# Probabilities of an attention stage: turned over DRAM and on VectorE instead of TensorE, and a new order of each engine's round

## The reference, cut to what matters

```python
kv_c, q_c = kv @ W_kvc, q @ W_dq
k_rope, q_rope = _rope(kv_c @ W_kr, lk), _rope(q_rope, lq)
scores = (einsum('bhqd,bkhd->bhqk', q_nope, k_nope) + einsum('bhqr,bkr->bhqk', q_rope, k_rope)) * scale
good = (k_ids <= qs) & (k_ids >= qs - LOOKBACK)
attn = softmax(where(good[:, None, :, :], scores, NEG), axis=-1)
out = einsum('bhqk,bkhd->bqhd', attn, v).reshape(b, lq, H * HD)
return out @ W_o
```

## Time and profile before

| | us |
|---|---|
| median of 3 runs | 3070.87 |
| lowest, highest | 3063.78, 3072.26 |
| the profiled execution, its own time | 3065.81 |
| its span in the profile | 3064.0 |
| PE, DVE, ACT, POOL busy in it | 3032.5, 2248.4, 1379.9, 1224.1 |

### The profile page before, as it was taken

One profiled execution on the slowest core, in us unless ns is written; L12 is line 12 of the kernel. 1 busy time (PEld: TensorE's weight loads), 2 busy tenths in 40 slices (PEclk: granted clock), 3 DMA queues, 4 the chain that ended last, 5 costly groups with the idle time before them and its releaser, 6 DMA issues.

```text
span 3064.0 us, 50062 instructions
## 1 busy us (share of the span) xinstructions
PE 3032.5 (99%) x18181; PEld 2636.4 (86%) x18181; DVE 2248.4 (73%) x5504; ACT 1379.9 (45%) x3399; POOL 1224.1 (40%) x1190
## 2 busy tenths in 40 slices
PE   9999999999999999999999999999999999999999
PEld 6777777899899799999999999999998788888887
DVE  7989999755677788888888888888887533333342
ACT  4655555433566455555555555555555211111111
POOL 9999999454333433333222333333311111111120
PEclk9999999999999999999999999999999999999999
DMA  4444442298899511111111111111102211111110
GB/s 153 131 144 138 129 130 86 86 307 299 220 265 284 189 49 49 49 49 43 49 42 49 49 49 36 49 38 47 49 29 81 88 56 55 55 49 43 46 42 14
DMA packets 179011, 292.41 MB, mean 95 GB/s; under 512 B 22616, under 2 KB 73952, under 8 KB 178768
## 3 DMA queue, kind: packets, MB, share of 16 engines
q1 hardware_dynamic: 145200, 193.24, 20.4%
q0 software_dynamic: 23344, 77.35, 7.9%
q10 hardware_dynamic: 10224, 18.62, 1.6%
HBM read 177.38 MB, written 111.76 MB: 94 GB/s over the span
## 4 chain that ended last, share of the span: by engine, by line
PE 92%; DVE 3%; DMA 2%; POOL 1%; ACT 1%; issue 1%; SPq 0%; POOLq 0%; DVEq 0%
PE f_Y L559 4%; PE t_U L1818 4%; PE f_Y L560 4%; PE f_Y L562 4%; PE t_U L1819 4%; PE t_U L1820 4%; PE g_O L2640 4%; PE g_PH L2628 4%; PE g_PH L2627 4%; PE g_PH L2626 4%; PE g_O L2642 4%; PE g_O L2641 4%; PE t_T L1794 3%; PE f_Y L554 2%; PE t_PO L1804 2%; PE t_PO L1805 2%
## 5 line engine op out<-in xcount | busy, mean ns | idle before, releaser
L1954 ACT ACTIVATE t_pr<-t_sm,t_nb 128x256 f32<-128x256 f32 x512 | 256.7, 502 | 418.5 <-DVE t_nb L2176 418.5
L2372 POOL TENSOR_TENSOR t_r<-t_r 128x256 f32<-128x256 f32 x128 | 95.8, 749 | 696.7 <-DVE t_r L2155 387.5
L2696 DVE CAST g_hh<-g_hf 128x512 fp32r<-128x512 f32 x128 | 67.8, 530 | 382.0 <-PE g_O L2642 380.2
L2667 ACT ACTIVATE g_hf<-g_PH,b1g 128x512 f32<-128x512 f32 x128 | 88.1, 688 | 528.3 <-PE g_PH L2628 457.0
L1360 POOL TENSOR_TENSOR c_kf<-c_vt,c_ct 128x512 f32<-128x512 f32 x256 | 284.5, 1129 | 5.9 <-ACT c_vt L775 3.2
L2186 DVE TENSOR_SCALAR t_pr<-t_pr,t_rw 128x256 f32<-128x256 f32 x512 | 256.7, 501 | 18.1
L559 PE MATMUL f_Y<-c_kh,c_th 128*128 128x512 f32 x540 | 250.8, 465 | 0.0
L562 PE MATMUL f_Y<-c_kl,c_th 128*128 128x512 f32 x540 | 213.7, 396 | 0.7 <-DVE c_kl L1072 0.7
L560 PE MATMUL f_Y<-c_kh,c_tl 128*128 128x512 f32 x540 | 213.4, 395 | 0.0
L2640 PE MATMUL g_O<-g_w,g_hh 128*128 128x512 f32 x512 | 200.1, 391 | 5.0 <-DVE g_hl L2698 5.0
L1818 PE MATMUL t_U<-t_voh,t_oth 128*128 128x512 f32 x512 | 202.0, 394 | 0.0
(11 more groups left out here) (375 smaller groups left out, 9974.9 us busy)
## 6 DMA issues: line engine op xcount, KB each, us to landing
xs<-c_zero SPq DMA_DIRECT2D x71, 256.0 KB, 4.6
f_xg<-xs SPq DMA_DIRECT2D x284, 64.0 KB
ys<-f_yt ACTq DMA_DIRECT2D x71, 256.0 KB, 5.1
f_xg<-xn SPq DMA_DIRECT2D x40, 256.0 KB, 4.9
c_xt<-x SPq DMA_DIRECT2D x32, 256.0 KB, 3.5
c_cr<-ctx SPq DMA_DIRECT2D x32, 256.0 KB, 4.0
...
```

## The change

It has these parts.

- PE's `pturn` is gone, with its bank T, which becomes the second bank of PO. The probabilities of head N are normalised by ACT (`normalise(N)`, in ACT's round N+1, a copy scaled by the reciprocal) into `pr` in another order of columns. SP writes them to DRAM (`fp`), waits for that, and reads them back as `pq`. DVE turns them in blocks of 32x32 into `ptq` (`pturn(N)`, in DVE's round N+2). ACT makes `pth` from it. The low part is made by GpSimd for even heads, in its round N+2, and by DVE for odd heads, at the start of its round N+3 (`plow`).
- `av` moves from round N+2 to N+3 on PE, `vo` from N+4 to N+5; `oth` and `otl` have two buffers instead of three, and their ACT and DVE steps move to round N+4.
- In each engine's round the chain of the probabilities comes first. `qabs` of DVE moves from the end of the even round to the odd round behind it.
- The result is stored by SP in four pieces, two rounds later than GpSimd did it, and the residual is loaded in four pieces a round later. The rows come in the order of the turned blocks. x2 of batches 2 and up is kept by GpSimd's queue. GpSimd's mix is spread over rounds 11 to 14.
- `krf` shares memory with `kc`, so DVE's `krope` waits for `kvp`.
- At the seam, the first block of the dense stage (`dense_first(0, 0)`) is put on PE ahead of the last `vo`, the rows of group 1 move two steps earlier on SP, and the first dense weights are split a round later.

The diff, cut to its core:

```diff
 def sync_attention:
+    def store(b):
+        w.wait_ge(*V["add", 2 * b + 1])
+        for c in range(4):
+            sp.dma_start(turned_rows_of(d["x3"][b], c), m.xo[32 * c:32 * c + 32, :, :]).then_inc(*Q["to"]("out", b, c))
+    def probabilities(N):
+        w.wait_ge(*A["nm", 2 * N + 1])
+        w.wait_ge(*V["pt", N - 4])
+        sp.dma_start(d["fp"][N % 4].rearrange("(i p f) -> p i f", i=4, f=128),
+                     m.pr[:, N % 2, :, :, :, :].rearrange("p i k t f -> p i (k t f)")).then_inc(*Q[f"ps{N % 2}"]("ps", N))
+        w.wait_ge(*Q[f"ps{N % 2}"]["ps", N])
+        w.wait_ge(*V["pt", N - 2])
+        sp.dma_start(m.pq[:, N % 2, :], d["fp"][N % 4].rearrange("(p l) -> p l", p=128)).then_inc(*Q[f"pl{N % 2}"]("pl", N))
...
+        if N >= 6 and (N - 6) % NH == NH - 1:
+            store((N - 6) // NH)
+        if 5 <= N < TOTAL and (N - 5) % NH == (12 if N - 5 < NH else 8):
+            residual((N - 5) // NH)
...
+        if N < TOTAL:
+            probabilities(N)
 def tensor_attention:
-    def pturn(N):
-        w.wait_ge(*V["nm", 2 * N + 1])
-        w.wait_ge(*V["ptl", N - 1])
-        for kb in range(2):
-            for t in range(2):
-                i = pe.transpose(m.T[...], m.pr[:, N % 2, t, 128 * kb:128 * kb + 128], ident)
     def av(N):
-        w.wait_ge(*V["ptl", N])
-        w.wait_ge(*V["otl", N - 1])
+        o = m.PO[N % 2][:, 0:256]
+        w.wait_ge(*(V if N % 2 else G)["ptl", N])
+        w.wait_ge(*V["otl", N - 2])
...
+        if N >= 5:
+            vo(N - 5)
...
+        if 3 <= N <= TOTAL + 2:
+            av(N - 3)
+        if N == TOTAL + 2:
+            dense_first(pe, w, K, 0, 0)
 def scalar_attention:
+    def normalise(N):
+        w.wait_ge(*Q[f"ps{N % 2}"]["ps", N - 2])
+        for t in range(2):
+            x, k4 = 2 * N + t, (2 * N + t) % 4
+            w.wait_ge(*V["rc", x])
+            ac.activation(m.pr[:, N % 2, :, :, t, :], m.sm[:, k4, :].rearrange("p (i k f) -> p i k f", i=4, k=2), ACT.Copy,
+                          scale=m.rw[:, k4, 1:2]).then_inc(*A("nm", x))
     def pturn(N):
-        w.wait_ge(*P["pt", N])
+        w.wait_ge(*V["pt", N])
...
+        if 4 <= N <= TOTAL + 3:
+            av(N - 4)
+        if 1 <= N <= TOTAL:
+            normalise(N - 1)
         if N < TOTAL:
             exps(N)
+        if 2 <= N <= TOTAL + 1:
+            pturn(N - 2)
 def vector_attention:
     def pturn(N):
+        w.wait_ge(*Q[f"pl{N % 2}"]["pl", N])
+        w.wait_ge(*P["av", N - 2])
+        ve.transpose(m.ptq[:, N % 2, :, :].rearrange("p k q -> p (k q)").rearrange("p (k c t) -> p c k t", k=4, c=4),
+                     m.pq[:, N % 2, :].rearrange("p (c k f) -> p c k f", c=4, k=4)).then_inc(*V("pt", N))
+    def plow(N):
         w.wait_ge(*A["pth", N])
...
+        if 3 <= N <= TOTAL + 2 and N % 2 == 0:
+            plow(N - 3)
         if N < TOTAL:
             maxima(N)
+        if 2 <= N <= TOTAL + 1:
+            pturn(N - 2)
+        if N < TOTAL and N % 2 and (N + 1) // 2 < TOTAL // 2:
+            qabs((N + 1) // 2)
+        if 4 <= N <= TOTAL + 3:
+            av(N - 4)
...
+            inverses(N)
+        if N >= 5 and (N - 5) % NH == NH - 1:
+            add_rows((N - 5) // NH)
 def gpsimd_attention:
+    def pturn(N):
+        w.wait_ge(*A["pth", N])
+        gp.tensor_tensor(m.ptl[:, N % 2, :, :], m.ptq[:, N % 2, :, :], f32(m.pth[:, N % 2, :, :]), ALU.subtract).then_inc(*G("ptl", N))
...
+        if 2 <= N <= TOTAL + 1 and N % 2 == 0:
+            pturn(N - 2)
```

More of the change, by code:

```diff
@@ L277, in attention_memory @@
     m.pth = t("pth", [128, 2, 2, 256], F32R)
+    with ExitStack() as low:
+        m.ptq = sb(nc, low, "t_ptq", [128, 2, 2, 256])
     m.ptl = t("ptl", [128, 2, 2, 256], F32R)
-    m.oth = t("oth", [128, 3, 256], F32R)
-    m.otl = t("otl", [128, 3, 256], F32R)
+    m.oth = t("oth", [128, 2, 256], F32R)
+    m.otl = t("otl", [128, 2, 256], F32R)
     m.sm = t("sm", [128, 4, 256])
-    m.pr = t("pr", [128, 2, 2, 256])
+    m.pr = t("pr", [128, 2, 4, 2, 2, 32])
+    m.pq = t("pq", [128, 2, 512])
     m.wkh = t("wkh", [128, 2, 128], F32R)
@@ L1553, in every_other_head, with turned_rows_of, kept @@
     return qr[half, q4 % 2, :, :].rearrange("p (i z) c -> p z i c", z=2)[:, z, :, :]
+def turned_rows_of(ap, c):
+    return ap.rearrange("(t u c) l -> u c t l", t=2, c=4)[:, c, :, :]
+def kept(b):
+    return "tx2" if b < 2 else "tx3"
 def halves_of(ap):
@@ L1593, in residual @@
         if b:
-            w.wait_ge(*Q["to"]["out", b - 1])
+            w.wait_ge(*Q["to"]["out", b - 1, 3])
         else:
@@ L1633, in sync_attention @@
     segment(1)
-    for N in range(TOTAL + 4):
+    for N in range(TOTAL + 7):
         b, h = divmod(N, NH)
-        if N >= 4 and (N - 4) % NH == (12 if N - 4 < NH else 8):
-            residual((N - 4) // NH)
+        if N >= 6 and (N - 6) % NH == NH - 1:
+            store((N - 6) // NH)
+        if 5 <= N < TOTAL and (N - 5) % NH == (12 if N - 5 < NH else 8):
+            residual((N - 5) // NH)
         if N < TOTAL and b + 2 < B:
@@ L1642, in sync_attention @@
                 segment(b + 2)
-                keep(b + 2)
         if N + EARLY + 2 < NH:
@@ L1852, in tensor_attention @@
     weights(7)
-    for N in range(TOTAL + 4):
+    for N in range(TOTAL + 5):
         b, h = divmod(N, NH)
@@ L2252, in vector_attention @@
                 qrot(q4 + 1, 1)
-        if N >= 4 and (N - 4) % NH == NH - 1:
-            add_rows((N - 4) // NH)
+            inverses(N)
+        if N >= 5 and (N - 5) % NH == NH - 1:
+            add_rows((N - 5) // NH)
         if b + 1 < B:
@@ L2377, in turned, with keep @@
         gp.tensor_tensor(m.xTl[:, :, c], rows_whole(m)[:, :, c], f32(m.xTh[:, :, c]), ALU.subtract).then_inc(*G("xl", b, t))
-    def store(b):
-        w.wait_ge(*V["add", 2 * b + 1])
-        gp.dma_start(halves_of(d["x3"][b]), m.xo[:, :, :]).then_inc(*Q["to"]("out", b))
+    def keep(b):
+        w.wait_ge(*G["mix", b, 0])
+        w.wait_ge(*G["mix", b, 1])
+        gp.dma_start(halves_of(d["x2"][b]), m.xt[:, :, :]).then_inc(*Q["tx3"]("x2", b))
+    def pturn(N):
+        w.wait_ge(*A["pth", N])
+        gp.tensor_tensor(m.ptl[:, N % 2, :, :], m.ptq[:, N % 2, :, :], f32(m.pth[:, N % 2, :, :]), ALU.subtract).then_inc(*G("ptl", N))
     w.wait_ge(*K.PE["m2", TILES - 1])
@@ L2405, in gpsimd_attention @@
         q4, r = divmod(N, 4)
+        if 2 <= N <= TOTAL + 1 and N % 2 == 0:
+            pturn(N - 2)
+        if b + 2 < B:
+            if h == 10:
+                gather(b + 2, 0)
+            if h == 11:
+                mix(b + 2, 0, (0,))
+            if h == 12:
+                mix(b + 2, 0, (1,))
+                gather(b + 2, 1)
+            if h == 13:
+                mix(b + 2, 1, (0,))
+            if h == 14:
+                mix(b + 2, 1, (1,))
+                keep(b + 2)
+        if b + 1 < B:
+            if h == (0 if b else 3):
+                power(b + 1, 0)
+            if h == (1 if b else 4):
+                power(b + 1, 1)
         if N < TOTAL:
@@ L2572, in sync_dense_begin @@
     m, P, V, Q = K.g, K.P, K.V, K.Q
-    w.wait_ge(*Q["to"]["out", 1])
+    w.wait_ge(*Q["to"]["out", 1, 3])
     w.wait_ge(*P["qcp", B - 1])
@@ L2648, in tensor_dense @@
         g, k = divmod(n, BLOCKS)
-        if n < DSTEPS:
-            first(g, k)
+        if 0 < n < DSTEPS:
+            dense_first(pe, w, K, g, k)
         if n >= 2:
```

155 lines of the change are left out of this document (60 added, 95 removed).

## The result

| | before | after |
|---|---|---|
| median of 3 runs, us | 3070.87 | 3149.93 |
| lowest, highest | 3063.78, 3072.26 | 3149.43, 3158.37 |
| profiled execution, its span | 3065.81, 3064.0 | 3158.37, 3156.6 |
| start of keys (PE) for batches 0, 2 and 15 | 1000.6, 1138.7, 2201.2 | 999.7, 1144.1, 2272.3 |
| mean period of a batch, from the start of keys for batch 2 to that for batch 15 | 81.73 | 86.78 |

The ratio is 1.0272, interval 1.0237 to 1.0308: the changed kernel is slower by 2.7%, where a gain of 1.6% was forecast. The period was to fall by 3.1 us and rose by 5.05; 13 of them make 65.7 of the 92.6 us between the two spans. (The profiled execution of the changed kernel is the longest of its three; between the medians lie 79 us.) Another 5.4 are lost ahead of the keys for batch 2, 4.5 between the last keys and the last scores, and 17.0 from there to the end.

The account below looks back on a forecast made before the run. PE, busy in all 81.73 us of a batch, was the bound; 74.7 plus waits gave 78.65, a gain of 3.1. Fourteen batches (43) and the ends made 46 us, so 3022 us, range 3000 to 3042 (chance 0.42).

Parts of the forecast that it names:

- The floor: PE in an attention batch: taking away 16 heads' turns, 7.0 of 81.73 us, leaves 74.7.
- Rival A: Attention batches: transfers hide and GpSimd is no hindrance, 76.6 us a batch, 2990 in all (2960 to 3000); chance 0.22.
- term 1: PE before scores: waits for the pair's low part behind DVE's maxima and turn, 1.3 and 0.3 us a batch.
- DVE's and ACT's load: Attention batch: DVE busy 68.2 of 74.7 us with turns at 1.08, ACT 13 more on some 45; both fit.
- So I charge nothing for them: SP's queue: round 10's loads are through before head 10 is normalised, so they cost its transfers nothing.
- Term 6: SP's queue: residual and store in four pieces go ahead of a head's transfer, 0.5 us a batch, from 0 to 2.
- The landing of 4.85 us: Each head's trip through DRAM: write 2.35, read 2.4, semaphores 0.1; bounds 4.8 and 5.5, more in traffic.
- B: Rival: landings of 5.5 us and over make even heads' wait exceed DVE's slack; 3070 to 3095 us, slower; chance 0.14.
- Term 5: GpSimd's queue: even low parts meet rotation, mixes and gathers; PE waits 0.7 in round 9, 0.5 in round 14.
- Terms 1 and 2: PE's wait before scores (term 1), and DVE's wait for even heads' transfers, about 0.9 twice in four heads, paid from slack.
- Term 7: SBUF port: DVE's odd low parts, both operands in SBUF, may wait for GpSimd; 0.3 us a batch, at most 1.5.
- The ends: Outside batches 1 to 14: batch 0 gains 3 us, the last batch 2, the end after the last head loses 2.

Follow-up runs that it names:

- e12: Changed kernel with turn to projection and next batch's rope turns a round later, absorbed queries' low part before the turn, GpSimd reordered and relieved: 2983.53 us.
- e1: Changed kernel without the probabilities' transfers through DRAM; DVE turns ACT's buffer directly: 2995.24 us, ratio 0.9778 to the kernel before.
- e5: Changed kernel without the round 10 loads of rows and context (1 MB), from batch 2 on: 3128.64 us.
- e2: Changed kernel with all 512 transfers issued, but DVE turns ACT's buffer without waiting for the read: 3096.11 us.
- e13: e2 with GpSimd's rope sums ahead of gathers and mixes, and low parts of heads 8, 10 and 12 on DVE: 3042.44 us.
- e10: Changed kernel with each head's write but no read back; DVE's turn waits for the write and takes ACT's buffer: 3045.65 us.
- e8: Changed kernel with turn to projection and rope turns a round later, GpSimd's sums first, absorbed queries' low part before the turn, bulk in pieces: 3076.60 us.
- e14: Changed kernel with GpSimd's rope sums first, low parts of heads 8, 10 and 12 on DVE, absorbed queries' low part before the turn: 3126.01 us.

## Why the prediction was wrong, by its own steps

**The floor** held. PE's stream without the turns was put at 74.7 us; e12 runs at 75.04. Rival A, transfers hidden, was put at 76.6 a batch and 2990 us; e1, which has no transfers, shows 76.9 and 2995. The number agrees by luck in part: A kept the waits of term 1, and in e1 PE never waits before scores for `qal`; it waits 8.2 us from 1232 to 2272 us for ACT ahead of query compression, and 1.8 for GpSimd. As a total, what the reordering costs was estimated rightly.

**DVE's and ACT's load** held too. DVE was to be busy 68.2 us a batch and is for 63.2 to 65.5, mostly since the turn takes 0.71 us in place of 1.08. The row of the dense stage was the wrong one to take. The kernel before has the same instruction in its expert stage too, at 711 ns:

```profile
L1288 DVE STREAM_TRANSPOSE f_xq<-f_xg x71: 704/711/715, 778.9 to 986.1; 128x512 f32<-128x512 f32 x71
```

The three places read in the same order. The expert stage and the new turn write 32 elements in a row (`c t`), the dense stage steps by four elements (`t c`). The scaled copies were taken at 0.41 and are 0.507, just over the 0.4 to 0.5 given; ACT had room. These are the rows of the changed kernel (busy us, mean ns, idle before) that answer to the earlier trace rows:

```profile
L2218 DVE STREAM_TRANSPOSE t_ptq<-t_pq 128x512 f32<-128x512 f32 x256 | 181.6, 709 | 184.8 <-DMA t_pq<-fp 183.7
...
L1982 ACT ACTIVATE t_pr<-t_sm,t_rw 128x256 f32<-128x256 f32 x512 | 232.5, 507 | 15.0 <-DVE t_rw L2213 10.6
```

**"So I charge nothing for them"** is the step that failed first: the loads of round 10, said to be through before head 10 is normalised. The write was issued 2.7 us after them and landed 3.9 us late. Nor did the prediction count the gathers issued just ahead of it, which alone leave it at 4.2 us (e5). **Term 6**, residual and store ahead of a head's transfer, had 0.5 us with bounds 0 to 2; the write is 2.8 us late with residual and gathers ahead, 1.2 to 1.4 with the residual alone (batches 14 and 15), and 1.6 behind the store. The landing of 4.85 us was right in half of the rounds (2.3 and some 2.7) and 9 us in the worst. I had asked what the median transfer takes, and the bounds came from rows in which no 1 MB stood ahead. In terms of the rivals the mean landing was that of B: 3.0 us from a write to the issue of its read, and a read of some 2.7 (its medians by round in e5 are 2.6 to 3.0). The median of all 256 writes is 2.4; the 2.9 of the profile's page is over the 128 of odd heads, the only ones whose landing it has. B ended at 3094: it let each late microsecond cost only 0.375 of a microsecond per head, as if all heads were late alike, while e5 gives about 1 where one head is late alone.

**No term for what the transfers do to others** was the larger gap. The sum asked when the new transfers land, and never when the old ones do. Gathers went from 3.5 to 6.1 us, and with them GpSimd's queue; e2 has 101 us without any wait of the turn for the landing, and e13 gives 54 of them back by relief of GpSimd's queue. Term 5 gave GpSimd 0.7 + 0.5 us a batch, decided in part by "the gathers' landing" as it was. PE's waits for GpSimd in the changed kernel are (15.3 + 12.0) / 12 = 2.3 us a batch, for the rope sums and the low parts; the one named, `t_xTl`, isn't among them.

**Terms 1 and 2** had the places partly right. PE waits before scores for `qal`, but 21 times in 12 batches and up to 2.5 us, not 0.4 us in nearly every round of kinds 2 and 0. In e1, with no landing to wait for, this wait is absent, so all of it in the changed kernel hangs on landings; that the faster turn is what keeps it away in quiet rounds is likely and wasn't tried. DVE waits for `t_pq` 90 times in 12 batches, up to 5.8 us, in odd rounds too.

**Term 7**, the port, was 0.3 with 1.5 at most. DVE's low part with both operands in SBUF has a mean of 807 ns where its quiet value is 682: 8 x 0.125 = 1.0 us a batch. DVE's timeline, and the GpSimd instructions beside it:

```profile
1554.52 1.33 DVE L2223 TENSOR_TENSOR t_ptl<-t_ptq,t_pth 128x512 fp32r<-128x512 f32 x1
...
1564.91 0.71 DVE L2218 STREAM_TRANSPOSE t_ptq<-t_pq 128x512 f32<-128x512 f32 x1 [1.53 <-DMA t_pq<-fp]
```

```profile
1554.02 1.28 POOL L2379 TENSOR_TENSOR t_xt<-t_xt,t_xT 128x512 f32<-128x512 f32 x1
...
1564.24 1.27 POOL L2421 TENSOR_TENSOR t_ptl<-t_ptq,t_pth 128x512 fp32r<-128x512 f32 x1
```

The low part takes 1.33 us beside GpSimd's addition, and no more than 0.69 in the 69 cases in which GpSimd computes nothing; the turn beside the same kind of instruction takes its 0.71, and all 256 turns lie between 700 and 715 ns. That is what the Trainium skill (SBUF — State Buffer, Who interferes with whom) says of one and of two inputs in SBUF.

**The clock** was called a risk without a sign. In the gap that head 10 makes it became a cost. The 1.4 us worked out above are of one batch. From 1232 to 2272 us the granted clock is 0.985 in the changed kernel and 1.00 before: 0.015 x 1040 = 15 us in 12 batches, some 1.3 a batch, as an estimate from above, since PE is idle in a part of it.

**The ends** were to gain 3 us. Ahead of the keys for batch 2, 5.4 are lost instead of 3 gained, and from the last scores to the end 17.0 for the 2 gained. There the last head's trip isn't all, and DVE's wait for it isn't needed: this stretch is 17.3 us longer than before in e2 too, where DVE waits for no landing, 16.2 in e10, and 4.4 in e1. In the changed kernel SyncE sends dense weights only behind the last read, and PE starts the last `vo` after a wait with its clock at half. The chain and the windows of the changed kernel:

```profile
2427.30 2.44 DMA fp<-t_pr
...
2430.60 3.72 DMA g_stg<-f1w
2434.35 0.63 ACT g_w L2509
```

```profile
2437.00:2442.00 5.00, 4.23 (x13) 3.66 (x14) 1.74 (x4) 0.90 (x2) 0.00 (x0) 0.50 0.01 3
```

e12 has this end as well (19.1 us longer than before); it wasn't mended.

The loss of some 83 us divides, by the ratios and in round numbers: a gain of 68 by the reordering and the turns taken off PE (e1), 98 by what the transfers do without any wait of the turn (e2), 53 by DVE's wait for the landing (changed kernel over e2). Of the 98, over half is GpSimd's queue behind late gathers (e13) and some 13 lie at the end; the rest isn't assigned. The parts aren't additive in the remedies, as e8, e12 and e14 show.
